# One image more resident and a different order of mean and squares in a two-pass convolution kernel

## The reference

```python
def reference(x, weight):                     # weight: (64, 64, 1, 1)
    v = group_norm(x, groups=32, eps=1e-5)    # mean and variance over 2 channels x 65536 pixels
    xc = clip(v, -8, 8)
    s = max(max(abs(xc)), 1e-8) / 127         # one scale for the whole tensor
    xq = clip(round(xc / s), -127, 127) * s
    ws = max(mean(abs(weight), axis=(1, 2, 3)), 1e-8)
    wq = clip(round(weight / ws), -1, 1) * ws
    return x + conv1x1(xq, wq)
```

## Time and profile before

| | before |
|---|---|
| median of 3 runs | 1868.37 us (1868.13 to 1868.42) |
| the profiled execution | 1868.27 us |
| its span, first to last instruction | 1866.5 us |
| busy in the span: PE, DVE, ACT, POOL | 57%, 72%, 58%, 24% |
| moved by DMA | 795.00 MB, 426 GB/s over the span |
| read from HBM, written | 526.42 MB, 268.44 MB |
| chain that ended last: DMA, DVE, ACT | 65%, 16%, 6% |

### The profile page before, as it was taken

How to read it: one execution, slowest core, us unless ns; L and a number is a source line. 1 busy time by engine, 2 the same in 40 slices (tenths; PEclk the granted TensorE clock), 3 DMA queues, 4 the chain that set the end, 5 groups by cost and what they waited for, 6 DMA issues and landing times.

```text
span 1866.5 us, 10231 instructions
## 1 busy us (share of the span) xinstructions
PE 1061.7 (57%) x2239; PEld 313.8 (17%) x2239; DVE 1336.5 (72%) x711; ACT 1086.7 (58%) x797; POOL 451.9 (24%) x380
## 2 busy tenths in 40 slices
PE   0999999999999646533333433334333433344332
PEld 0333333333333211100000000000000000000000
DVE  4999999999999979846555665566555665566553
ACT  0999999999999757634444444434443444434441
POOL 0777777777777400000000000000000000000000
PEclk9999999999999855555555555555555555555555
DMA  9999999999999999999999999999999999999998
GB/s 407 429 427 428 428 429 429 428 428 428 429 428 428 428 351 429 430 431 431 431 431 431 432 431 431 430 432 431 431 431 431 431 431 431 430 432 431 431 431 368
DMA packets 55035, 795.00 MB, mean 426 GB/s; under 512 B 6256, under 2 KB 6256, under 8 KB 6256
## 3 DMA queue, kind: packets, MB, share of 16 engines
q1 hardware_dynamic: 36144, 526.40, 66.3%
q10 hardware_dynamic: 18880, 268.48, 33.6%
HBM read 526.42 MB, written 268.44 MB: 426 GB/s over the span
## 4 chain that ended last, share of the span: by engine, by line
DMA 65%; DVE 16%; ACT 6%; issue 4%; POOL 2%; another core or an unknown queue 2%; PE 2%; SPq 0%; ACTq 0%; DVEq 0%; POOLq 0%
DMA out_dram<-ring 36%; DMA ring<-in_x_dram 29%; DVE square_maxs L486 7%; DVE ring L594 6%; ACT ring L319 3%; POOL levels L295 2%; ACT levels L422 2%; PE product L637 1%; DVE levels L588 1%; DVE first_sq_maxs L496 1%; ACT levels L401 0%; ACT product L312 0%; PE product L633 0%; ACT product L336 0%
## 5 line engine op out<-in xcount | busy, mean ns | idle before, releaser
L674 PE MATMUL product<-levels,w_lhsT 128*128 128x512 bf16 x1024 | 483.3, 627 | 705.6 <-DVE levels L588 705.6
L422 ACT ACTIVATE levels<-ring,tile_affine 128x2048 int16<-128x2048 f32 x240 | 490.8, 2090 | 582.7 <-DMA ring<-in_x_dram 568.5
L594 DVE SCALAR_TENSOR_TENSOR ring<-product,out_scale,ring 128x2048 f32<-128x2048 f32 (+1 forms) x258 | 600.8, 2329 | 0.1
L486 DVE TENSOR_REDUCE square_maxs<-ring 128x4096 f32 (+1 forms) x119 | 522.8, 4416 | 34.7 <-ACT ring L319 34.6
L588 DVE TENSOR_SCALAR levels<-levels 128x2048 bf16<-128x2048 int16 (+1 forms) x258 | 176.6, 684 | 445.0 <-ACT levels L422 434.3
L295 POOL TENSOR_TENSOR levels<-ring 128x512 f32<-128x512 f32 x360 | 449.5, 1278 | 182.2 <-DMA ring<-in_x_dram 179.7
L319 ACT ACTIVATE ring<-ring,group_stats 128x4096 f32<-128x4096 f32 x119 | 440.4, 3701 | 0.0
L637 PE MATMUL product<-levels,neg_mean 128*128 128x512 f32 x720 | 364.8, 617 | 12.6
L674 PEld LDWEIGHTS product<-levels,w_lhsT 128*128 128x128 bf16 x1024 | 110.2, 130 | 1078.2 <-DVE levels L588 823.5
L633 PE MATMUL product<-ring,neg_mean 128*128 128x512 f32 x480 | 236.5, 615 | 3.1 <-DMA ring<-in_x_dram 2.1
L637 PEld LDWEIGHTS product<-levels,neg_mean 128*128 128x128 f32 x720 | 118.4, 189 | 240.2 <-POOL levels L295 206.8
(11 more groups left out here) (82 smaller groups left out, 56.2 us busy)
## 6 DMA issues: line engine op xcount, KB each, us to landing
ring<-in_x_dram SPq DMA_DIRECT2D x251, 2048.0 KB, 15.2
out_dram<-ring ACTq DMA_DIRECT2D x126, 2048.0 KB, 44.7
out_dram<-ring ACTq DMA_DIRECT2D x4, 1024.0 KB, 5.6
levels<-in_L_conv_weight_dram ACTq DMA_DIRECT2D x2, 16.0 KB, 8.4
```

Source lines behind the costliest of these rows:

```text
L422: nc.scalar.activation(levels[:, h, :], halves[:, 2 * s + h, :], ACT.Identity, bias=tile_affine[:, a, 1, :], scale=tile_affine[:, a, 0, :] ...
L486: nc.vector.tensor_reduce(square_maxs[:, bass.ds(k + 1, 1)], ring[:, slot1(REST + g), :], AX_X, ALU.max).then_inc(maxed, 1)
L594: nc.vector.scalar_tensor_tensor(part, product[:, h, at], out_scale[:, :], part, ALU.mult, ALU.add).then_inc(combined, 1)
L674: mm = pe.matmul(product[:, h, n * BANK:(n + 1) * BANK], w_lhsT[:, :], ints[:, h, n * BANK:(n + 1) * BANK], start=True, stop=True)
```

## The change

`KEPT` goes from 5 to 7 and `RING1` from 7 to 5; the twelve slots stay. `REST` becomes 1, the loop's turn 10 chunks after the first ten, eleven turns in place of eight. ACT does mean and squares of the same chunk in turn, no longer one ahead. The kept chunks are squared in 14 pieces of 2048 columns: four among the first ten chunks (after `g` = 2, 4, 6, 8), then one in each of the ten first turns. ACT, no longer DVE, adds eps to the variances (`variances`, Identity); DVE weighs the maxima with a plain reciprocal of the variance (`largest_of`), and reciprocal roots are made for image 0 alone at first (`reciprocal_roots(1, 0, 1)`), for the 120 other chunks while chunk 4 of the second pass is due (`affine_of_rest`, with the matmul of `picked` moved there). The scale needs one reciprocal less in its chain. In the second pass a half of chunk 0 or 1 is stored behind the activation of the half two units later, not ahead of it.

```diff
-KEPT = 5
-RING1 = 7
+KEPT = 7
+RING1 = 5
 RING2 = 8
 SLOTS = RING1 + KEPT
-TURN = 2 * RING1
-PRE = 8
+TURN = 10
+PRE = 10
+PIECE = 2048
+FIRST_PIECES = [2, 4, 6, 8]
...
             def squares_of_kept(j):
+                if not (isinstance(j, int) and j == 0):
+                    act.wait_ge(kept_maxed, j)
                 nc.scalar.activation(kept_squares, kept_parts[:, bass.ds(j, 1), :], ACT.Square,
...
-            def roots(n, first, cols):
+            def variances(n, first, cols):
                 act.wait_ge(var_made, n)
-                nc.scalar.activation(std[:, first:first + cols], var_ps[:, first:first + cols], ACT.Sqrt,
-                                     scale=-1.0, bias=eps[:, :]).then_inc(std_guess, 1)
+                nc.scalar.activation(var_eps[:, first:first + cols], var_ps[:, first:first + cols], ACT.Identity,
+                                     scale=-1.0, bias=eps[:, :]).then_inc(var_kept, 1)
...
-            close(0, 0)
             for g in range(PRE):
-                close(g + 1, 0)
+                close(g, 0)
                 squares(g, 0)
-                if g == 1:
-                    squares_of_kept(0)
+                if g in FIRST_PIECES:
+                    squares_of_kept(FIRST_PIECES.index(g))
             with act.Fori(0, TURNS - 1) as t:
                 for g in range(PRE, PRE + TURN):
-                    close(g + 1, t)
+                    close(g, t)
                     squares(g, t)
                     if g == PRE + 1:
-                        squares_of_kept(t + 1)
-            for g in range(PRE, PRE + TURN - 2):
-                close(g + 1, TURNS - 1)
+                        squares_of_kept(t + len(FIRST_PIECES))
+            for g in range(PRE, PRE + TURN - 1):
+                close(g, TURNS - 1)
                 squares(g, TURNS - 1)
-                if g == PRE + 4:
-                    roots(1, 0, SOON)
-            squares(PRE + TURN - 2, TURNS - 1)
+                if g == PRE + 3:
+                    variances(1, 0, SOON)
+                    act.wait_ge(var_kept, 1)
+                    nc.scalar.activation(std[:, 0:1], var_eps[:, 0:1], ACT.Sqrt).then_inc(std_guess, 1)
             close(PRE + TURN - 1, TURNS - 1)
             squares_of_last()
-            roots(2, SOON, TURN)
+            variances(2, SOON, TURN)
...
-            store_half(0, 0)
             for c in range(1, TC):
...
                 for h in range(2):
-                    act.wait_ge(multiplied, EXTRA + (2 * c + h - 1))
+                    act.wait_ge(multiplied, 2 if c == 1 and h == 0 else EXTRA + (2 * c + h - 1))
                     nc.scalar.activation(levels[:, h, :], halves[:, 2 * s + h, :], ACT.Identity,
                                          bias=act_affine[:, 1, 0:1], scale=act_affine[:, 0, 0:1]).then_inc(scaled, 1)
-                    if c == 1:
-                        store_half(h, 1 - h)
-                    elif c == 2 and h == 0:
-                        store_half(1, 1)
-                if c > 2:
+                    if c <= HALVED:
+                        store_half(c - 1, h)
+                if c > HALVED:
                     store(0, c - 1)
+                if c == 2:
+                    act.wait_ge(var_kept, 2)
+                    nc.scalar.activation(std[:, 1:N1 + 1], var_eps[:, 1:N1 + 1], ACT.Sqrt).then_inc(std_guess, 1)
...
+            then(nc.vector.tensor_scalar(w_small[:, 4:5], w_small[:, 1:2], 0.5 / QMAX, None, ALU.mult))
...
+            def largest_of(n, first, cols):
+                at = slice(first, first + cols)
+                dve.wait_ge(var_kept, n)
+                then(nc.vector.reciprocal(recip_var[:, at], var_eps[:, at]))
+                then(nc.vector.tensor_tensor(square_maxs[:, at], square_maxs[:, at], recip_var[:, at], ALU.mult))
+                then(nc.vector.tensor_reduce(largest_so_far[:, n - 1:n], square_maxs[:, at], AX_X, ALU.max))
+            def reciprocal_roots(n, first, cols):
+                at = slice(first, first + cols)
                 dve.wait_ge(std_guess, n)
-                then(nc.vector.tensor_scalar(var_eps[:, at], var_ps[:, at], -1.0, GN_EPS, ALU.mult, ALU.add))
-                then(nc.vector.reciprocal(work[:, 0, at], std[:, at]))
-                then(nc.vector.tensor_tensor(work[:, 1, at], work[:, 0, at], var_eps[:, at], ALU.mult))
-                then(nc.vector.tensor_tensor(work[:, 0, at], work[:, 1, at], std[:, at], ALU.add))
-                then(nc.vector.reciprocal(half_rstd[:, at], work[:, 0, at]))
-                nc.vector.tensor_tensor(rstd_square[:, at], half_rstd[:, at], half_rstd[:, at],
-                                        ALU.mult).then_inc(stats_ready, 1)
+                then(nc.vector.reciprocal(var_eps[:, at], std[:, at]))
+                then(nc.vector.tensor_tensor(double_rstd[:, at], std[:, at], recip_var[:, at], ALU.mult))
+                nc.vector.tensor_tensor(double_rstd[:, at], double_rstd[:, at], var_eps[:, at],
+                                        ALU.add).then_inc(stats_ready, 1)
                 dve.wait_ge(stats_ready, n)
...
             for g in range(PRE, PRE + TURN - 1):
                 maxima(g, TURNS - 1)
...
-                elif g == PRE + 6:
-                    statistics(1, 0, SOON)
-                    largest_of(0, 0, SOON)
+                if g == PRE + 3:
+                    largest_of(1, 0, SOON)
+                    reciprocal_roots(1, 0, 1)
...
-            dve.wait_ge(squared, USES + 1)
-            statistics(2, SOON, TURN)
-            largest_of(1, SOON, TURN)
+            largest_of(2, SOON, TURN)
...
             def affine_of_rest():
+                reciprocal_roots(2, 1, N1)
+                dve.wait_ge(picked, 1)
+                for i in range(2):
+                    at = picked_ps[:, i * N1:(i + 1) * N1].rearrange("p (t k) -> p t k", k=TC)
+                    then(nc.vector.tensor_tensor(by_row[:, i, :, :], at, own, ALU.mult))
...
-            pe.wait_ge(stats_ready, 2)
-            pe.matmul(picked_ps, pick[:, :], group_stats[:, :, :].rearrange("p s n -> p (s n)"),
-                      start=True, stop=True).then_inc(picked, 1)
...
+                        if isinstance(t, int) and t == 0 and c == 4 and h == 0:
+                            pe.wait_ge(combined, u)
+                            pe.wait_ge(stats_ready, 2)
+                            pe.matmul(picked_ps, pick[:, :], group_stats[:, :, 1:N1 + 1],
+                                      start=True, stop=True).then_inc(picked, 1)
```

More of the change, by code:

```diff
@@ L78, in preact_quant_conv_kernel @@
         halves = ring[:, :, :].rearrange("p s (h f) -> p (s h) f", h=2)
-        kept_parts = ring[:, RING1:SLOTS, :].rearrange("p s f -> p (s f)").rearrange("p (t e) -> p t e", e=KEPT_PART)
+        kept_parts = ring[:, RING1:SLOTS, :].rearrange("p s f -> p (s f)").rearrange("p (t e) -> p t e", e=PIECE)
         levels = sb("levels", [P, 2, HALF], I16)
@@ L141, in preact_quant_conv_kernel @@
         pair_junk = product[:, 1, :]
-        kept_squares = product[:, :, :].rearrange("p h f -> p (h f)")[:, 2 * HALF - KEPT_PART:2 * HALF]
+        kept_squares = product[:, :, :].rearrange("p h f -> p (h f)")[:, 2 * HALF - PIECE:2 * HALF]
         var_ps = banks[:, 2, 0:N1 + 1]
-        picked_ps = banks[:, 3, 0:2 * (N1 + 1)]
+        picked_ps = product[:, 1, 0:2 * N1]
         row_ps = banks[:, 0, 0:P]
@@ L160, in preact_quant_conv_kernel @@
         kept_squared = sem("kept_squared")
+        kept_maxed = sem("kept_maxed")
         first_merged = sem("first_merged")
@@ L495, in maxima_of_kept @@
                 dve.wait_ge(kept_squared, j + 1)
-                return nc.vector.tensor_reduce(first_sq_maxs[:, bass.ds(j + REST, 1)], kept_squares, AX_X, ALU.max)
-            half_rstd = group_stats[:, 1, :]
-            rstd_square = work[:, 1, :]
-            def statistics(n, first, cols):
+                nc.vector.tensor_reduce(first_sq_maxs[:, bass.ds(j + REST, 1)], kept_squares, AX_X,
+                                        ALU.max).then_inc(kept_maxed, 1)
+            double_rstd = group_stats[:, 1, :]
@@ L512, in statistics @@
                 dve.wait_ge(stats_ready, n)
-            def largest_of(n, first, cols):
-                at = slice(first, first + cols)
-                then(nc.vector.tensor_tensor(work[:, 0, at], square_maxs[:, at], rstd_square[:, at], ALU.mult))
-                then(nc.vector.tensor_reduce(largest_so_far[:, n:n + 1], work[:, 0, at], AX_X, ALU.max))
             for i in range(REST):
@@ L547, in _ @@
             dve.wait_ge(maxed, USES)
-            nc.vector.scalar_tensor_tensor(largest[:, :], tail_max[:, :], rstd_square[:, N1:N1 + 1],
+            nc.vector.scalar_tensor_tensor(largest[:, :], tail_max[:, :], recip_var[:, N1:N1 + 1],
                                            largest_so_far[:, 0:1], ALU.mult, ALU.max).then_inc(rows_maxed, 1)
-            own = own_chunk[:, :].rearrange("p (t k) -> p t k", t=1).broadcast_to([P, TILES - 1, TC])
```

(16 more changed lines are left out.)

43 lines of the change are left out of this document (22 added, 21 removed).

## The result

The changed kernel takes 1877.94 us (median of 5 runs, 1875.01 to 1879.39), the kernel before beside it 1868.37 (5 runs, 1868.13 to 1870.27): the ratio is 1.0047, with an interval of 1.0034 to 1.0059. By the medians it is slower by some 9.6 us; the forecast was 9.3 faster. The profiled execution, the slowest of the five, took 1879.39 us, its span 1877.6, which is 11.1 more than before.

What follows compares the result with a forecast made beforehand. The kernel was taken as bound by DMA transfers, with one hole between the passes. The terms -9.7 + 4.0 + 0.4 - 4.0 = -9.3 us gave 1859.0 us from a profiled 1868.27, range 1855 to 1866.5.

Steps and rivals of the forecast that it cites:

- the ring of five suffices: First pass, steady: five slots turn over in 24.5 us, leaving 10.3 for issue and landing, where a load needs 7.6.
- My first rival: First pass: the ring of five starves in every turn, 1865 at 9.0 us issue to landing, 1876 at 10; chance 0.13.
- Bytes: Whole kernel: two chunks fewer are loaded, taken as -9.7 us.
- Start: First pass, start: ACT's backlog and the early pieces make loads late, taken as +4.0 us, bounds 2.8 and 6.
- Steady state: First pass, loop: ACT's 4.63 us and DVE's 4.33 + 0.2 per chunk stay hidden under the loads' 4.89; no cost.
- Last turn: First pass, last turn: six DVE operations after its fourth chunk take 3.6 us; cost +0.4 us, bounds 0 and 2.
- Between the passes: From last landing to first stores: the hole shrinks from 8.5 to 4.0 us, 0.5 lost behind; -4.0, bounds -1 and -6.

Runs made afterwards that it cites:

- e8: The kernel before (ring of seven) with one load per turn held back by two more maxima; 1894.98 us, ratio 1.0138.
- e11: The kernel before with one load per turn, the one at `PRE + 8`, held back by one more maximum; 1870.92 us, ratio 1.0008.
- e3: The changed kernel without the ten kept pieces of the loop, neither their squares nor their maxima; 1862.31 us, ratio 0.9976.
- e15: The kernel before with six loads in a row of each turn (indices 8 to 13) held for one more maximum; 1878.23 us, ratio 1.0055.
- e4: The changed kernel with kept pieces of 1024 columns, eight among the first ten chunks, then two per turn; 1864.47 us, ratio 0.9976.
- e1: The changed kernel with six chunks kept and a ring of six, turn of 12; 1858.50 us, ratio 0.9948.
- e6: The changed kernel with six chunks kept, a ring of six and pieces of 1024 columns; 1858.06 us, ratio 0.9939.
- e2: The changed kernel with five chunks kept and a ring of seven, so only order, weighing and stores differ from before; 1860.43 us, ratio 0.9957.

## Why the prediction was wrong

**The step that failed** is "So in the steady state the ring of five suffices, with 2.7 us to spare". Three numbers stood in it. A slot was to be held 14.1 us; it is held 14.66 (chunk landed at 157.12, next load of its slot issued at 171.78), since I counted from POOL's start and not from the landing (0.15), left out the handover from DVE to SP (0.18), and had the wait for the mean and the one before the maximum too short (0.10 and 0.12). A piece was to delay the next load by 1.8 us; it is 1.6. These leave 8.15 in place of 8.5 and would have done no harm with a load of 7.6. The third is the one that broke: 7.6 us from issue to landing, read off the first loads of the kernel. It is a true number for a queue with nothing in it (e8), and not what a load needs to land on time behind one that is still under way: there it took 8.0 to 9.9 (e11) and, in the changed kernel's late loads behind the pieces, 9.1 to 10.6.

The Trainium skill, DMA: Bandwidth & Descriptors, section "Anatomy of one DMA — SWDGE (gpsimd) path", gives a fixed 2.0 us plus bytes at 436 GB/s, fitted per DMA issued by GpSimd (these are issued by SP); for 2 MB that is an estimate of 6.8. e8's 7.6 is near it, the 10.5 of the changed kernel's load is not, and there the measurement decides.

My first rival was this mechanism ("Where issue to landing needs over 8.5 us, each microsecond more is lost once a turn"), with 1876 at 10 us. It had a chance of 0.13 because I took the start's 7.6 as evidence against it, though the trace of before had no load in its first pass that was issued late into a running stream; the 9.0 of the earlier trace rows was the only row of that kind and spoke for the rival. That the rival's 1876 lies so near is partly chance: it is eleven turns of 1.5 us, while the trace has nine of about that size and some 4 us with other causes (below). Its break-even is also misreckoned: with eleven turns, 9.3 us are used up at 8.5 + 9.3 / 11 = 9.35 us, not at 9.6.

**Term by term.** The span grew by 11.1 us:

- *Bytes*: two loads fewer, 249, and the second pass's rate as before. -9.7 holds.
- *Start*: POOL begins the 22nd chunk of the stream at 157.27; before, at 151.74. So +5.5, not +4.0. The period of ACT was to be 4.43 and is 4.53: from mean to squares 0.82 (162.31 to 163.12) against 0.59 in the earlier trace rows, so the wait costs 0.23 and not 0.12; 13 chunks by 0.1 are 1.3 of the 1.5. I had taken it from a single wait in the earlier trace rows, with 0.3 as the upper bound.
- *Steady state*: costed at nothing. From 157.27 on, before's 98 further landings would have ended at 636.8; they ended at 655.5, 18.7 later. With the last landing's 1.5 (below) taken off, **+17.2**. Nine turns with a piece lie in it (the tenth piece, behind the twelfth chunk, is in the start). At the landings behind the pieces some 13 us are lost, 1.5 a turn; 2.8 follow the two falls of the clock, and 1.3 are one landing behind an instruction fetch (last section). e3, without the loop's pieces, gets 15.6 us back in all.
- *Last turn*: +0.4 forecast, +1.5 measured (the last pitch is 6.4). DVE's operations took 4.65 us (638.46 to 643.11), not 3.6, as these rows show, the last of which stands in the second pass, where POOL does nothing:

```profile
639.33 1.36 DVE L513 TENSOR_TENSOR square_maxs<-square_maxs,recip_var 128x111 f32<-128x111 f32 x1
...
641.88 1.19 DVE L522 TENSOR_TENSOR group_stats<-group_stats,var_eps 128x1 f32<-128x1 f32 x1
...
700.50 0.28 DVE L521 TENSOR_TENSOR group_stats<-square_sums,recip_var 128x120 f32<-128x120 f32 x1
```

  One column costs 1.19 us there, 120 columns 0.28 here. The rule of the Trainium skill's SBUF — State Buffer, section "SBUF: two separate sides", that a DVE operation with two SBUF inputs and one of GpSimd exclude each other for a whole instruction, agrees, and its +2 was nearer to the 1.5 than my +0.4.
- *Between the passes*: quantising at T + 17.6 and stores at T + 23.4, 26.7, 29.9 and 32.8 were forecast as 17.6, 23.4, 26.8, 30.0 and 33. DVE's work for the 120 columns delays it by 4.4 us (699.58 to 703.93) where some 4 were expected. The hole is 56 x (1 - 402/430) = 3.6 us where 4.0 were reckoned; a store's data start 0.87 us after its issue (first packet at 679.72), not 1.2. The sum needs -3.4 for this term, not -4.0, so about 1 us more is lost elsewhere. The packets show it: I had the last chunk's data in 1.75 us before T, as before the change, with the next load's data moving from then on. At T the kernel before had moved 1.4 us' worth of data beyond its last chunk, the changed kernel, whose last load came late, only 0.4.

-9.7 + 5.5 + 17.2 + 1.5 - 3.4 = +11.1.

**What stays open.** Why a load that comes late into a stream with nothing behind it takes up to 3 us more than one into an empty queue. Each load leaves sixteen completion marks in the trace, as many as there are DMA engines, and I take them as one for each; worked out from them, from issue on:

```
run, load issued at    first engine after    last engine after    between
after      171.78            7.96                 9.79              1.82
after      178.30            6.84                10.47              3.62
e8         200.86            6.74                 7.59              0.85
e11        187.95            6.88                 7.99              1.11
e11        463.49            6.81                 9.87              3.06
e15        192.11            8.09                 9.42              1.33
```

In four rows the first mark comes after the same 6.7 to 6.9 us; in the first and the last it comes later, which I read as engines that still had the load before in hand. It is the last mark that is late, and in the changed kernel the engines do not all stop: the window from 180 to 190 has a DMA share of 0.95, and from 178 to 192 the packets show at least 12 under way at every half microsecond, where e8 has none for 2.05 us. That engines which restart one by one are slower than engines which start together is argued from this table, not shown: no run set the spread alone, and the two loads of e11, issued with about the same lead, differ by 1.9 us without a reason that I found.

## What to carry to other kernels

A ring's slack has to be reckoned with the time that a load needs in a running stream, with another one always queued behind it: here two transfers, 9.8 us, sufficed and 8.15 did not, while the 7.6 of an empty queue looked like ample room. What counts is the one worst delay in a turn, so work beside the ring goes in small pieces (e4), and where the ring is short a slot more in it (e1, e6: 1858 us, the fastest of all) is worth more than a load saved; where it is not short, the load saved is (e2 against e1, 2 us). An edit with several parts is worth splitting: order, weighing and stores alone (e2) gave 8.2 of the 10 us that e1 and e6 gained.

## What the runs showed of the hardware

- Issue to landing of the same 2 MB: 7.6 us with the queue empty, 8.0 to 9.9 for one late load, 9.1 to 10.6 for the late ones of the changed kernel; 15.2 in a queue three deep.
- TensorE's granted clock fell to the lower level (0.50) behind two late landings of the changed kernel, for 3.4 and 6.8 us, where PE waited 2.3 and 2.4 us for a chunk; behind the other late landings of its loop it stayed at 1.00. In e8, where each held load lands some 3.4 us late, it fell in every turn of the loop. So a starved ring can be starved further by the engine that it kept waiting: the late chunk at the second fall had its mean 7.9 us after landing, against 5.2 for the late chunks of the turns without a fall.
- The page lists packets of instructions (instruction fetches) among the DMA queues, and late landings follow some of them. In the kernel before, the sixteen marks of a load lie within 0.56 us of each other until 87 us. Fetches pass at 90.73 (8 KB) and 95.64 (16 KB, 1.1 us); the marks are 1.0 us apart at 92, 1.9 at 98, with two late landings there (pitches of 5.4 and 5.7) though the queue is full, and 1.75 apart still at 440. In the changed kernel the late landing at 259.1 follows a fetch at 253.47 (16 KB, 1.0 us), and its load had been issued in time, 9.9 us ahead of when it was due; the landings at 200.6 in e3 and at 202.1 in e4, also issued 9.9 ahead and 1.2 to 1.3 late, follow fetches of 16 KB at 198.43 and 199.51. Others, such as those of before at 601.01 and 610.52, made no landing late. No run moved a fetch, so that it causes the delay is argued from this order in time.
